# Attention's right sides prepared early and spilled in two parts, C's low part on VectorE, and an earlier second x

## The reference, cut to what matters

```python
K      = c @ W_mem.T                       # memory_proj, 1024 wide
attn   = softmax(x @ K.T / 32)
ctx    = attn @ K
gate   = sigmoid(x @ G1.T + ctx @ G2.T + b_gate)   # W_gate = [G1 | G2]
fused  = x + gate * ctx
out    = fused * rsqrt(mean(fused**2) + 1e-6) * norm_w
```

## Time and profile before

| | |
|---|---|
| median of 3 runs | 943.36 us (941.61 to 944.84) |
| the profiled execution, its own time | 944.35 us |
| its span in the profile | 942.5 us |
| TensorE busy (PE) | 98% |
| VectorE busy (DVE) | 80% |
| ScalarE busy (ACT) | 44% |
| GpSimd busy (POOL) | 10% |
| DMA, mean | 164 GB/s, 155.00 MB |
| mean granted clock of TensorE | 0.996 |

### The profile page before, as it was taken

The page is one execution under the profiler, slowest core; times in us unless marked ns, Lnnn a source line. Parts: engine busy times, 40 slices in busy tenths (PEclk is TensorE's granted clock), DMA queues, the critical chain, the costliest instruction groups (busy, mean ns, idle before and its releaser), DMA issues.

```text
span 942.5 us, 13107 instructions
## 1 busy us (share of the span) xinstructions
PE 924.0 (98%) x5084; PEld 806.1 (86%) x5084; DVE 750.1 (80%) x995; ACT 419.1 (44%) x652; POOL 93.1 (10%) x90
## 2 busy tenths in 40 slices
PE   9989999999999999999999989999999999999996
PEld 8878888888888888999999968888888888888884
DVE  5975566665665579778878989999999999999987
ACT  5442222222222225444446665555556565555553
POOL 0000000000000000000000112222222222122212
PEclk9999999999999999999999999999999999999998
DMA  9432432244223454845543715555454555545542
GB/s 353 159 135 90 134 135 89 90 126 143 90 90 114 163 214 156 292 143 190 173 166 113 269 66 201 201 199 182 176 184 168 184 182 194 169 179 196 201 179 90
DMA packets 35086, 155.00 MB, mean 164 GB/s; under 512 B 3664, under 2 KB 5712, under 8 KB 25936
## 3 DMA queue, kind: packets, MB, share of 16 engines
q1 hardware_dynamic: 34736, 153.63, 46.9%
q10 hardware_dynamic: 288, 0.52, 0.2%
HBM read 110.10 MB, written 44.04 MB: 164 GB/s over the span
## 4 chain that ended last, share of the span: by engine, by line
PE 87%; DVE 6%; DMA 2%; issue 2%; ACT 1%; SPq 1%; POOL 0%; DVEq 0%; POOLq 0%; ACTq 0%
PE psum L1200 29%; PE psum L1202 29%; PE psum L1201 29%; DMA g_raw<-in_g 1%; DVE g_l L715 1%; DMA k_spill<-k_out 1%; PE psum L1282 1%; DMA xs_raw<-in_xt 0%; DVE wb_l L715 0%; DVE wn_l L715 0%; DVE k_out L836 0%; SPq L263 0%; DVE g_raw L743 0%; DVE g_raw L760 0%; DVE g_raw L755 0%
## 5 line engine op out<-in xcount | busy, mean ns | idle before, releaser
L1200 PE MATMUL psum<-g1h,xh 128*128 128x512 f32 x448 | 175.0, 391 | 2.6 <-DVE z L826 2.6
L1201 PE MATMUL psum<-g_l,xh 128*128 128x512 f32 x448 | 175.0, 391 | 0.0
L1201 PE MATMUL psum<-wb_l,th 128*128 128x512 f32 x448 | 174.8, 390 | 0.0
L1200 PEld LDWEIGHTS psum<-g1h,xh 128*128 128x128 f32 x448 | 84.5, 189 | 20.8 <-issue 3.4
L1202 PE MATMUL psum<-g1h,xs_l 128*128 128x512 f32 x256 | 100.3, 392 | 0.0
L1201 PEld LDWEIGHTS psum<-g_l,xh 128*128 128x128 f32 x448 | 84.4, 188 | 17.7
L448 ACT ACTIVATE xh<-xs_raw 128x512 fp32r<-128x512 f32 x64 | 40.2, 632 | 129.6 <-PE psum L1202 123.2
L1201 PEld LDWEIGHTS psum<-wb_l,th 128*128 128x128 f32 x448 | 84.3, 188 | 15.9
L409 POOL TENSOR_TENSOR c_l<-c_raw,c_h 128x1024 fp32r<-128x1024 f32 x16 | 39.1, 2444 | 578.5 <-ACT c_h L448 578.5
L826 DVE TENSOR_TENSOR z<-psum,bias 128x512 f32<-128x512 f32 x64 | 44.3, 692 | 62.5 <-PE psum L1202 62.5
L1092 DVE TENSOR_TENSOR zb<-psum,zb 128x512 f32<-128x512 f32 x112 | 76.4, 683 | 3.0 <-PE psum L1202 2.0
(11 more groups left out here) (172 smaller groups left out, 2393.2 us busy)
## 6 DMA issues: line engine op xcount, KB each, us to landing
xs_raw<-in_xt SPq DMA_DIRECT2D x16, 1024.0 KB, 6.5
z_spill<-z SPq DMA_DIRECT2D x16, 1024.0 KB, 8.7
zb<-z_spill SPq DMA_DIRECT2D x16, 1024.0 KB, 6.4
xrow<-in_x SPq DMA_DIRECT2D x30, 512.0 KB, 7.2
out<-xrow SPq DMA_DIRECT2D x30, 512.0 KB, 3.4
xb_raw<-in_xt SPq DMA_DIRECT2D x8, 1024.0 KB, 8.5
xa_raw<-in_xt SPq DMA_DIRECT2D x8, 1024.0 KB, 4.8
y_spill<-y SPq DMA_DIRECT2D x16, 512.0 KB, 9.2
```

The lines of the kernel that those rows point to most:

```text
L1200: nc.tensor.matmul(tile, ah, mh, start=start, stop=False, skip_group_check=True)
L1201: nc.tensor.matmul(tile, ah, ml, start=False, stop=False, skip_group_check=True)
```

## The change

Four things change; the computed values are the same.

1. The 14 right-side blocks are prepared one per batch in batches 1 to 14 of X G1^T. SP loads one to three raw blocks into `wp_raw`, `wp_other`, `wp_third`; VectorE makes 0, 1 or 2 sums (`WP_SUMS`); ACT makes the high part, VectorE the low part; SP stores both (512 KB each) as `wbhd` and `wbld`. There is one set of places, so each load waits until the stores before it have landed. From Y's round 1 on the low parts are loaded, from the last round on the high parts, one block as each product of that round ends. The cuts, sums and raw loads of before go.
2. SP's list at the change from X G1^T to Y: `xb`, `wq0` are issued after the last of those stores has landed; VectorE's and ACT's lists there are put in a new order (sums earlier, `y_cut(3)` and two W copies moved), and `zb[0]` is loaded before the last Y store.
3. C's low part is made on VectorE. In attention's batch 0 ACT's copy for C of batch 1 stands ahead of the second mem copy, where before it stood behind it.
4. The second x is loaded after fold step 6 (`fold_mm` 7), ahead of the k stores. The second `k_out` moves to another place.

```diff
-        k_out = [at(f"k_out{i}", [PART, 2, D], F32, (193, 163)[i]) for i in range(2)]
+        k_out = [at(f"k_out{i}", [PART, 2, D], F32, (193, A21_AT)[i]) for i in range(2)]
+        wp_raw, wp_l = raw_low("wp", [PART, 2, BANK], A21_AT)
+        wp_other = at("wp_other", [PART, 2, BANK], F32, A21_AT + 4)
+        wp_h = at("wp_h", [PART, 2, BANK], F32R, 201)
+        wp_third = at("wp_third", [PART, 2, BANK], F32, 201)
...
+        WP = [0, 1, B22, T1, T3, T2, T4]
+        WP_FROM = {0: [(0, 0)], 1: [(1, 0)], B22: [(1, 1)], T1: [(0, 1), (0, 0)], T3: [(1, 1), (0, 1)],
+                   T2: [(1, 1), (0, 1), (0, 0)], T4: [(1, 0)]}
+        WP_SUMS = {0: 0, 1: 0, B22: 0, T1: 1, T3: 1, T2: 2, T4: 1}
+        wp_blocks = [(m, i) for m in range(2) for i in WP]
+        N_WP = len(wp_blocks)
... (sync engine)
+            sp.wait_ge(fold_mm, 7)
+            sp.dma_start(xs_raw[1][:, :, :], xt[1]).then_inc(x_in[1], DMA)
             for i in range(2):
                 sp.wait_ge(k_act, 2 * i + 2)
                 sp.wait_ge(k_dve, 2 * i + 2)
                 sp.dma_start(kd[:, 2 * i:2 * i + 2, :], k_out[i][:, :, :]).then_inc(k_stored, DMA)
-            sp.wait_ge(k_stored, 2 * DMA)
-            sp.dma_start(xs_raw[1][:, :, :], xt[1]).then_inc(x_in[1], DMA)
+            def load_wp(n):
+                m, i = wp_blocks[n]
+                src = (wt, kd)[m]
+                if n >= 1:
+                    sp.wait_ge(wp_stored, 2 * DMA * n)
+                else:
+                    sp.wait_ge(k_stored, 2 * DMA)
+                for (e, d), place in zip(WP_FROM[i], (wp_raw, wp_other, wp_third)):
+                    sp.dma_start(place[:, :, :], src[:, 2 * e:2 * e + 2, HALF[d]]).then_inc(wp_in, DMA)
+
+            def store_wp(n):
+                m, i = wp_blocks[n]
+                sp.wait_ge(wp_low, n + 1)
+                sp.dma_start(wbhd[m, i], wp_h[:, :, :].bitcast(F32)).then_inc(wp_stored, DMA)
+                sp.dma_start(wbld[m, i], wp_l[:, :, :].bitcast(F32)).then_inc(wp_stored, DMA)
             for b in range(B):
+                if 1 <= b <= N_WP:
+                    store_wp(b - 1)
+                if b == N_WP:
+                    sp.wait_ge(wp_stored, 2 * DMA * N_WP)
+                    sp.dma_start(xb_raw[0][:, :, :], xt[1]).then_inc(xb_in[0], DMA)
+                    load_wq(0)
                 if b < B - 1:
                     sp.wait_ge(gx_mm, P7 * (b + 1))
                 if b + 2 < B:
                     sp.dma_start(xs_raw[b % 2][:, :, :], xt[b + 2]).then_inc(x_in[b % 2], DMA)
-                if b == B - 3:
-                    sp.dma_start(xb_raw[0][:, :, :], xt[1]).then_inc(xb_in[0], DMA)
-                    load_wq(0)
+                if b < N_WP:
+                    load_wp(b)
                 elif b == B - 2:
                     sp.dma_start(xa_raw[0][:, :, :], xt[0]).then_inc(xa_in[0], DMA)
                     load_wq(1)
...
+            load_wb_high(0)
+            load_wb_high(1)
             sp.wait_ge(s_mm, 1)
             sp.wait_ge(y_stored[0], 2 * DMA)
             sp.dma_start(yt_raw[:, :, :], yd[1]).then_inc(yt_in, DMA)
             sp.dma_start(ct_raw[:, :, :], ct[1]).then_inc(ct_in, DMA)
+            load_wb_high(2)
+            sp.dma_start(zb[0][:, :, :], zd[0]).then_inc(zb_in[0], DMA)
+            for i in range(3, P7):
+                load_wb_high(i)
             store_y(SB - 1)
-            sp.wait_ge(y_mm, Y_LAST)
-            sp.dma_start(zb[0][:, :, :], zd[0]).then_inc(zb_in[0], DMA)
... (ACT, X G1^T)
             for n in range(XH, GX_LAST):
                 x_cut_high(n)
-                if n == GX_LAST - P7 + 6:
-                    ws_cut_high(S2)
-                    ws_cut_high(S1)
+                if P7 <= n - XH < GX_LAST - P7 and (n - XH) % P7 == 4:
+                    wp_cut_high((n - XH) // P7 - 1)
... (VectorE, X G1^T, behind gx_out, x_sums and x_cut of product i)
+                if 1 <= b <= N_WP:
+                    sums = WP_SUMS[wp_blocks[b - 1][1]]
+                    if i == 3 and sums == 2:
+                        wp_sums(b - 1, 0)
+                    elif i == 4 and sums >= 1:
+                        wp_sums(b - 1, sums - 1)
+                    elif i == 5:
+                        wp_cut(b - 1)
                 if b == B - 1:
                     if i == 1:
                         y_sums(0, 0)
+                        y_sums(0, 1)
                     elif i == 2:
+                        y_sums(0, 2)
                         ws_sums(S1)
                     elif i == 3:
                         ws_sums(S2)
-                        y_sums(0, 1)
                     elif i == 4:
-                        y_sums(0, 2)
+                        ws_sums(S3)
                         y_cut(0)
                     elif i == 5:
+                        ws_sums(S4)
                         y_cut(1)
-                        ws_sums(S3)
-            ws_sums(S4)
             y_cut(2)
             ws_cut(0)
             ws_cut(1)
+            y_cut(3)
             y_sums(0, 3)
... (ACT, attention)
-                if b == 0:
-                    wb_cut_high(8)
-                    wb_cut_high(9)
-                else:
+                if b >= 1:
                     square(b - 1, 0)
                     square(b - 1, 1)
                 if b + 1 < B:
                     exps(b + 1)
-                    if b >= 1:
-                        c_cut_high(b + 1)
+                    c_cut_high(b + 1)
                 mem_copy(b, 2)
-                if b == 0:
-                    c_cut_high(1)
... (VectorE, attention)
                 z_out(b, 3)
+                if b + 1 < B:
+                    c_cut(b + 1)
```

More of the change, by code:

```diff
@@ L1 @@
 from contextlib import ExitStack
+from itertools import accumulate
 import concourse.bass as bass
@@ L104, in build @@
         wb_h = [[at(f"wb{m}_{i}h", [PART, 2, BANK], F32R, HIGH_AT[2 * i + m]) for i in range(P7)] for m in range(2)]
-        wb = [[raw_low(f"wb{m}_{i}", [PART, 2, BANK], LOW_AT[2 * i + m]) for i in range(P7)] for m in range(2)]
-        wb_raw = [[r for r, _ in row] for row in wb]
-        wb_l = [[lo for _, lo in row] for row in wb]
+        wb_l = [[at(f"wb{m}_{i}l", [PART, 2, BANK], F32R, LOW_AT[2 * i + m]) for i in range(P7)] for m in range(2)]
         yt_h = at("yt_h", [PART, KE, N], F32R, 149)
@@ L167, in build @@
         y_stored = [sem(f"y{p}_stored") for p in range(2)]
-        wb_in = [[sem(f"wb{m}_{i}_in") for i in range(4)] for m in range(2)]
-        wb_sum, wb_high, wb_low = sem("wb_sum"), sem("wb_high"), sem("wb_low")
+        wp_in, wp_sum, wp_high, wp_low, wp_stored = (sem("wp_in"), sem("wp_sum"), sem("wp_high"), sem("wp_low"),
+                                                     sem("wp_stored"))
+        wbh_in = [sem(f"wbh{i}_in") for i in range(P7)]
+        wbl_in = sem("wbl_in")
         yt_in, ct_in, c_in, norm_in = sem("yt_in"), sem("ct_in"), sem("c_in"), sem("norm_in")
@@ L227, in w_slice @@
             return tile[:, k // 4, :, part, k % 4, :]
-        WB_IN = [0, T3, B22, 1]
+        WP = [0, 1, B22, T1, T3, T2, T4]
[3 more added lines that the diff above has]
+        wp_blocks = [(m, i) for m in range(2) for i in WP]
+        wp_sums_by = list(accumulate(WP_SUMS[i] for _, i in wp_blocks))
+        wp_loads_by = list(accumulate(len(WP_FROM[i]) for _, i in wp_blocks))
+        N_WP = len(wp_blocks)
         def gx_banks(b):
@@ L323, in _, with load_wb_high, load_wb_low @@
                 sp.dma_start(zd[b], z[b % 2][:, :, :]).then_inc(z_stored[b % 2], DMA)
[L325 to L329, removed]
+            def load_wb_high(i):
+                sp.wait_ge(y_mm, Y_LAST - P7 + i)
+                for m in range(2):
+                    sp.dma_start(wb_h[m][i][:, :, :].bitcast(F32), wbhd[m, i]).then_inc(wbh_in[i], DMA)
+            def load_wb_low(i):
+                for m in range(2):
+                    sp.dma_start(wb_l[m][i][:, :, :].bitcast(F32), wbld[m, i]).then_inc(wbl_in, DMA)
             for p in range(2):
@@ L347, in _ @@
                     store_y(s - 1)
-                if s < 2:
-                    for n in range(4):
-                        load_wb(s, n)
+                    for i in ((), (0,), (1,), (2,), (3,), (4,), (5, 6), ())[s]:
+                        load_wb_low(i)
+            load_wb_high(0)
+            load_wb_high(1)
             sp.wait_ge(s_mm, 1)
@@ L405, in _ @@
                                channel_multiplier=1).then_inc(ident_done, 1)
[L407 to L410, removed]
             def root(b, nb):
@@ L432, in last_root @@
                                    ).then_inc(rstd_done, 1)
-            c_cut(0)
-            for b in range(B):
-                if b >= 1:
[L437 to L440, removed]
+            for b in range(B - 1):
+                for nb in range(NB):
+                    root(b, nb)
             for nb in range(NB):
@@ L484, in x_cut_high, with wp_cut_high @@
```

(32 more changed lines are left out.)

58 lines of the change are left out of this document (7 added, 51 removed).

## The result

The changed kernel takes 952.66 us (median of 6, 951.6 to 953.81), the kernel before 943.62 (6 runs). The ratio is 1.0097 with a 95% interval of 1.0085 to 1.0109: slower by 1.0%, or 9.0 us. The profiled execution has 952.82 us around a span of 951.0. The forecast was 949.0 in a range of 943 to 956, slower 0.73. In experiments 1 and 2 three executions of twenty were disturbed (1895.63, 1021.03 and 2381.98 us); the ratios leave them out, and without them the two medians would be at most 0.3 us lower.

The account below looks back on a forecast made before the run. TensorE was taken to bound every steady round, so only its pauses count. Terms -4.5 (second x), +0.5 (inside X G1^T), +9.3 (X G1^T to Y), +0.3 (attention's start) sum to +5.6: 949.0 us, range 943 to 956.

Parts of the forecast that it names:

- the last batch of X G1^T: Last batch before Y: a TensorE pause of +8.8 us waiting for xa, plus +1.9 for clock and product 5; forecast +10.7.
- the second x: Fold and batch 0/1: loading x earlier removes a 2.8 us pause and 1.7 us of half clock, -4.5 us.
- the start of attention: Attention's first batches: late c moves the mem wait, 0.6 us of later waits go, clock may cost 0.9; +0.3 us net.
- From X G1^T to Y: Stage boundary: xb, wq0, xa, wq1 wait for the last block's stores to land; +8.8, +1.9 and -1.4, sum +9.3 us.
- Inside X G1^T: Batches of X G1^T: added copies, cuts, sums and stores ahead of x loads cost +0.5 us, bounds 0 and +10.
- Rival C: X G1^T: x comes late in each batch behind one with sums, each losing 1 us or more; 951 to 958, chance 0.13.
- The new order of lists before Y: Y's start: VectorE's new order repairs the pause at y, leaving 0.3 of 1.7 us, so -1.4 us.
- 18 halves of 512 KB at 1.27: Start of attention: 18 queued transfers between ct(1) and c, 1.27 us each, so c lands at 544.9.
- rival D: Start of attention: c and what follows are later than the sum says, +4 us, 953; chance 0.10.
- The step before it: Start of attention: after c lands, ACT takes 1.0 us for C and 0.6 for mem, then product 4 starts.
- rival B: Start of attention gives all it has because c lands before 541; sum +0.7, 944.1 us; chance 0.14.
- C's cut: Attention: moving C's low part to VectorE frees it 0.6 us a batch, but TensorE sets the time: 0.

Follow-up runs that it names:

- experiment 1: Changed kernel with the last of the 14 right-side blocks left out of the preparation, xb and wq0 loaded as batch 13 ends: 943.81 us, ratio 0.9999.
- experiment 2: Changed kernel with all 14 blocks prepared one batch earlier (batches 0 to 13), k_out in four parts, nothing left out: 944.10 us, ratio 1.0007.
- experiment 3: Changed kernel with c of batch 1, then yt and ct of batch 2, ahead of the last two high parts, xrow, zb1, norm: 943.52 us, ratio 1.0001.
- experiment 4: Changed kernel with ACT's old order in attention's batch 0, C's copy behind the second mem copy: 953.88 us, ratio 1.0105 to the kernel before.
- experiment 5: Changed kernel with the loads of norm and zb1 moved right behind c of batch 1: 953.34 us, ratio 1.0124 to the kernel before.
- experiment 6: Changed kernel with the loads of norm and zb1 moved behind yt and ct of batch 2: 948.61 us, ratio 1.0070 to the kernel before.
- experiment 7: Changed kernel with the load of norm alone moved behind yt and ct of batch 2: 950.88 us, ratio 1.0094 to the kernel before.
- experiment 9: Kernel before with only the second x loaded after fold step 6, ahead of the k stores, and k_out moved: 940.16 us, ratio 0.9972.
- experiment 8: Changed kernel with all blocks one batch earlier and the new order of SP's list as attention starts: 934.51 us, ratio 0.9910 to the kernel before.
- experiment 10: Kernel before with only C's low part made on VectorE and GpSimd's cut removed: 943.43 us, ratio 0.9996.
- experiment 11: Kernel before with only the new order of VectorE's and ACT's lists between X G1^T and Y, loads as before: 942.15 us, ratio 0.9987.

## Why the prediction was right, and where it was off

The direction, and the place that decides it, were right; the sum was +5.6 and the runs show +9.0. Two terms were each off by about 1 us and cancel: the last batch of X G1^T was taken 1.0 too dear, and the second x 0.7 too good. That they cancel is luck. What is left is the start of attention, 3.6 us more than forecast.

**The direction and the main term.** "From X G1^T to Y" was the step that made it slower, and it is so by experiments 1 and 2. Piece by piece, from batch 14's end (347.64 + 0.23 - 10.88 = 337.0): the last cut ends at +1.7 (forecast 2.0), the stores take 3.95 (4.8), xa lands at +14.8 (16.7), the pause is 7.2 (8.8), and the slow stretch costs 2.5 (1.9 with product 5). Each piece of the transfer was taken a little long; the clock a little short. In the six traces that keep the last block in batch 14 (the changed kernel and experiments 3 to 7) this place costs 8.9 to 9.9 us. The Trainium skill (TensorE: Matmul & The Clock Gate, Part 1) says that an array left idle drops to 1.2 GHz. The trace agrees for a pause of this length: the clock was already at 0.50 while TensorE still stood, other than after the shorter pause of the kernel before.

```profile
351.00:353.00 2.00, 0.00 (x0) 0.00 (x0) 1.15 (x1) 0.00 (x0) 0.00 (x0) 1.00 0.85 250
353.40:355.00 1.60, 0.00 (x0) 0.00 (x0) 1.60 (x3) 0.00 (x0) 0.00 (x0) 0.50 1.00 425
```

**The second x.** -3.8 by the traces, -3.3 by experiment 9, forecast -4.5. The mechanism holds; what was missed is that VectorE is behind with G1's cuts in batch 0, which leaves a wait. And the half-clock stretch of 1.7 us was read from one execution: of the 24 of the kernel before beside experiments 8 to 11, twelve took 941.4 to 943.0 us at a mean granted clock of 0.996 or 0.997, and twelve 943.9 to 944.8 us, all but two of these at 0.994 or 0.995. That fits a stretch that comes in some executions and not in others (no trace of a quick one is there to show it); the profiled one, 944.35 us, is of the second kind, so its rows promise more than the median can give. TensorE's timeline of the changed kernel:

```profile
61.79 0.47 PE L1198 MATMUL psum<-g1h,xh 128*128 128x512 f32 x1 [0.51 <-DVE z L839]
```

**Inside X G1^T.** Two stores ahead of each x load cost 0.4 us in this trace, in two gaps near 315, and 0.3 to 1.4 us in those of experiments 2 to 8. Rival C (each batch behind one with sums loses 1 us or more, 8 in all) is ruled out.

**The new order of lists before Y.** -1.4 forecast, -1.4 by the traces of the two kernels, but 0.9 by that of experiment 11. The new order alone leaves 0.8 us there, as in the traces of experiments 2 and 8, which have no long pause in the batch before; 0.3 is left only behind that pause.

**Start of attention: the term that was off.** Forecast +0.3, measured +3.9. The step that failed is a size: "18 halves of 512 KB at 1.27". From ct(1), which lands at 522.45 + 4.8 = 527.25, to c at 553.45 there are 26.2 us, 1.46 a half. By the forecast's 22.9 c would have landed at 550.1. It is 3.3 later, because of the one trailing part of the load (experiments 5 to 7): fifteen of c's sixteen increments were there at 550.91, 0.8 us behind the forecast, and the last one 2.6 behind those. With the clock's fall (1.5 us, forecast 0.9 at most after absorption) this is rival D, "c and what follows are later than the sum says, +4: 953". The step before it held to the tenth: c lands, 1.0 and 0.6 later product 4 starts (555.18). Experiment 3, 9.1 us faster, shows that this whole loss of 9.4 hangs on the order of transfers, and 4 to 6 that it is c *and* yt. What I had as a way out, rival B, asked for c before 541 and was far off.

**C's cut.** Zero, as forecast, by experiment 10. The Trainium skill (SBUF — State Buffer, two separate sides) says that whichever of VectorE and GpSimd starts first holds the pair of ports that they share. The traces agree: 3.14 us beside GpSimd's cut, 1.28 for all 30 without it. Its removal is worth nothing while TensorE is busy for the whole round.

**What was not seen in the forecast:** that the cost is not in the idea. The second x and the order before Y did free 5.2 us (3.8 and 1.4), and two places of SP's list took them back. With both mended, the start of attention pays too: against the kernel before, the trace of experiment 8 loses 4.0 us less around batch 0/1, 0.9 less in Y's first round and 5.1 less at the start of attention, and 0.6 more elsewhere in X G1^T. That makes the 9 us.

## What to carry to other kernels

When a kernel prepares data ahead of time through one set of places, look at what stands behind the last round of it: here fourteen rounds cost 0.4 us together (0.3 to 1.4 in the other traces) and the wait for the last store's landing 9.7. When cuts are replaced by loads, add up the bytes issued between the moment a late transfer may start and the moment its reader asks, and order that list by due time; a reader's place in its engine's list only decides which pause is named. A ledger of pauses before and after, place by place, tells in one table which part of a change to keep.

## What the runs showed of the hardware that was not expected

After pauses of about 7 us (the changed kernel and experiments 2 to 7) the granted clock was 0.50 from the first matmul on; in the changed kernel 6 matmuls ran in 2 us until about 360, 5 us after TensorE had gone on. After the 2.8 us pause of the kernel before, the first four ran at full clock and the fall came behind them. The length of a short pause does not tell whether the clock falls: after pauses of 2.1 us there was no fall in the kernel before and in experiments 9 and 10, but there was one in experiment 11, whose longer pause of 2.6 us in batch 0/1 had none; nor had one of 2.4 in experiment 10. Two windows of experiment 11, behind its 2.1 us pause and around its 2.6 us one, and one of experiment 10, behind its 2.4 us pause:

```profile
543.50:546.50 3.00, 3.00 (x9) 2.33 (x8) 3.00 (x3) 3.00 (x5) 2.58 (x1) 0.50 0.00 0
67.00:74.00 7.00, 4.59 (x21) 3.51 (x20) 5.56 (x10) 1.39 (x3) 0.00 (x0) 1.00 0.06 8
69.50:74.00 4.50, 4.50 (x20) 3.72 (x21) 3.03 (x5) 0.63 (x1) 0.00 (x0) 1.00 0.14 24
```

A half cost 1.27 us in the kernel before and 1.46 in the changed one, counted from last increment to last. Counted by the fifteenth of each load's sixteen increments, from 526.91 for ct(1) to 550.91 for c, it is 1.33. In a stretch of 26 us in which the DMA share was 1.0, the sixteenth fell from 0.4 us behind the fifteenth to 2.6 behind. The reader waits for the slowest part, so here a sum of sizes came out too short. Why one part falls behind is open.
